# Routing slice cut on token rows by VectorE, first chunk's lookup readied early, other lookups moved among the pairs of the linear attention

## The reference, cut to what matters

```python
xn = (x - mu) * rsqrt(var + eps) * ln_gamma + ln_beta          # second norm, on LN(x)
tile_idx = argmax over 64 tiles, in the best cluster, of sign(xn) @ tile_sigs.T
x_slice = xn[8*tile_idx : 8*tile_idx + 8]                      # 8 numbers per token
tok_min, tok_max = x_slice.min(), x_slice.max()
tile_min, tile_max = min / max of these over all tokens of a tile     # over all 2048 tokens
u = clip((x_slice - tile_min[tile_idx]) / (tile_max - tile_min + 1e-8), 0, 1 - 1e-6)
gi = floor(16 * u)                                             # one of 16 cells
delta = (bases[tile, j, gi] + slopes[tile, j, gi] * x_local) * output_scale[tile]
out[token, 8*tile_idx + j] = delta[j]
```

## Time and profile before

| what | value |
|---|---|
| median of 3 runs | 2363.11 us (2361.16 to 2364.78) |
| the profiled execution | 2363.24 us, span of the trace 2361.5 us |
| PE busy | 2062.1 us, 87% of the span, 12078 matmuls |
| DVE busy | 1227.2 us, 52% |
| ACT busy | 746.9 us, 32% |
| POOL busy | 220.9 us, 9% |

### The profile page before, as it was taken

One profiled execution on the slowest core, in us unless ns is written; L12 is line 12 of the kernel. 1 busy time (PEld: TensorE's weight loads), 2 busy tenths in 40 slices (PEclk: granted clock), 3 DMA queues, 4 the chain that ended last, 5 costly groups with the idle time before them and its releaser, 6 DMA issues. The chain is left out here.

```text
span 2361.5 us, 29596 instructions
## 1 busy us (share of the span) xinstructions
PE 2062.1 (87%) x12078; PEld 987.3 (42%) x12078; DVE 1227.2 (52%) x2281; ACT 746.9 (32%) x1163; POOL 220.9 (9%) x164
## 2 busy tenths in 40 slices
PE   5885669697975499989999899999998999999998
PEld 3553233334343344434444444444444444444443
DVE  5554364757643455463666265644565356623332
ACT  4562231324341112322235223432244223511211
POOL 3630202120200000000000010001000000000000
PEclk7886769797966599999999999999999999999999
DMA  7224030302021222322111111111111111122321
GB/s 258 83 72 167 1 58 1 58 1 58 8 52 72 81 72 98 110 87 72 45 42 59 53 46 37 63 36 63 54 55 45 54 46 54 63 90 99 116 93 68
DMA packets 90978, 158.75 MB, mean 67 GB/s; under 512 B 44182, under 2 KB 55772, under 8 KB 86108
## 3 DMA queue, kind: packets, MB, share of 16 engines
q1 hardware_dynamic: 90844, 156.86, 20.7%
HBM read 128.52 MB, written 18.87 MB: 62 GB/s over the span
## 5 line engine op out<-in xcount | busy, mean ns | idle before, releaser
L1169 PE MATMUL ps<-arena 128*128 128x512 f16 (+1 forms) x4512 | 1018.3, 381 | 22.6 <-DVE arena L1932 12.9
L1169 PEld LDWEIGHTS ps<-arena 128*128 128x128 f16 x4512 | 436.4, 99 | 542.8 <-issue 48.5
L1877 PE MATMUL ps<-arena 128*128 128x512 f16 x1536 | 349.0, 383 | 29.5 <-DVE arena L1923 16.3
L1877 PEld LDWEIGHTS ps<-arena 128*128 128x128 f16 x1536 | 147.4, 98 | 207.4 <-issue 29.4
L1899 ACT ACTIVATE arena<-ps,arena 128x512 f32<-128x512 f32 x128 | 87.6, 684 | 362.4 <-PE ps L1169 362.1
L1932 DVE SCALAR_TENSOR_TENSOR arena<-arena,ps 128x512 f32<-128x512 f32 x128 | 87.8, 686 | 210.1 <-ACT arena L1899 209.5
L2486 ACT ACTIVATE arena<-ps 128x1024 f32<-128x1024 f32 (+3 forms) x128 | 90.1, 704 | 253.7 <-PE ps L2395 253.6
L2591 DVE CAST arena<-arena 128x1024 f16<-128x1024 f32 (+3 forms) x128 | 66.6, 520 | 149.8 <-ACT arena L2486 147.7
L2557 DVE TENSOR_REDUCE arena<-ps 128x2 f32<-128x256 f32 (+3 forms) x128 | 99.5, 819 | 65.1 <-PE ps L2339 65.1
L1960 DVE SCALAR_TENSOR_TENSOR arena<-ps,arena 128x512 f32<-128x512 f32 x64 | 44.0, 687 | 139.6 <-PE ps L1877 139.4
L1941 DVE SCALAR_TENSOR_TENSOR arena<-ps,arena 128x512 f32<-128x512 f32 x128 | 95.7, 748 | 39.5 <-PE ps L1169 39.3
(11 more groups left out here) (265 smaller groups left out, 2446.7 us busy)
## 6 DMA issues: line engine op xcount, KB each, us to landing
arena<-wug_dram SPq DMA_DIRECT2D x128, 512.0 KB, 3.3
arena<-wd_hi_dram SPq DMA_DIRECT2D x16, 1024.0 KB, 5.0
arena<-wd_lo_dram SPq DMA_DIRECT2D x16, 1024.0 KB, 7.2
arena<-arena SPq DMA_DIRECT2D x144, 64.0 KB, 2.1
wug_dram<-arena SPq DMA_DIRECT2D x4, 2048.0 KB, 15.4
arena<-_attn_hidden_states_dram SPq DMA_DIRECT2D x4, 1024.0 KB, 12.4
arena<-in_L_ffn_W_up_dram SPq DMA_DIRECT2D x8, 512.0 KB, 4.4
arena<-in_L_ffn_W_down_dram SPq DMA_DIRECT2D x4, 1024.0 KB, 7.7
```

What stands on the lines that cost most here:

```text
L1169: ins = pe.matmul(out, left[a](c), right[b](c), start=(at == 0), stop=(at == 3 * n - 1))
L1877: ins = pe.matmul(k.ps[:, bank, :], act[x][:, slot, cols], wd[y][:, f, :], start=(f == 0 and m == 0), stop=(f == 7 and m == 2))
```

## The change

1. **Slice on token rows.** `y` stays token-major and is not scaled. ACT takes the sign straight from the bank, with gamma as scale and beta as bias (4 activations fewer per chunk). The four spreading matmuls and the 16 gathering matmuls go. DVE multiplies each token row (128x512) by the one-hot broadcast over 8, and reduces it over the tiles to 8 numbers; the reduce reads elements 32 bytes apart. As the slice is of the unscaled row, PE fetches gamma and beta of the tile with four matmuls of 16 columns (two more DMAs put them into `table`), and DVE multiplies and adds them in `route_ends_vector`.
2. **Lookup of chunk 0 readied.** In both spline blocks the one-hot, its turn, the copy and the 256 columns of bases and slopes are done before the extremes are known; after them PE fetches three columns. The scaling of x is done ahead too, and in setup the wait for the two bias loads stands behind the norm's sums.
3. **Lookups of chunks 1 to 3 among the pairs**, in one bank (6), in three parts, at steps 3, 6, 8 and 11. The sums of the weighted values have one bank (5) instead of two. Everything of q and k stands one step earlier, and the refinement of the lengths comes before the last mask instead of after it.
4. **Values first.** In the feature stretch the values are made in blocks 0 to 3, the outputs from block 4 on. On SP the values' store and reads stand ahead of the last 12 feature copies.
5. Routing in the rounds: two picks at the end of a round, two at steps 1 and 2 of the next, the extremes at step 3 (before at step 1). The waits on registers go, POOL's loop is written out.

```diff
+def route_gain_tensor(k, pe, i, n, bank):
+    for u in range(TPC):
+        ins = pe.matmul(k.ps[:, bank, 256 + 2 * DSL * u:256 + 2 * DSL * (u + 1)], k.hot_t[:, u * P:(u + 1) * P],
+                        k.table[:, 260:276], start=True, stop=True)
 def route_sign_scalar(k, e, i, n, c, banks):
-    e.activation(y, token_columns(k.ps[:, banks[c % 2], :]), ACT.Identity, bias=k.beta[:, c:c + 1],
-                 scale=k.gamma[:, c:c + 1]).then_inc(s["r_y"], 1)
-    e.activation(token_columns(k.sgt[:, c, :]), y, ACT.Sign).then_inc(s["r_sign"], 1)
+    e.activation(k.sgt[:, c, :], k.ps[:, banks[c % 2], :], ACT.Sign, bias=k.beta[:, c:c + 1],
+                 scale=k.gamma[:, c:c + 1]).then_inc(s["r_sign"], 1)
-def route_pick_vector(k, V, i, n, c, banks):
-    e.tensor_tensor(y, token_columns(k.ps[:, banks[c % 2], :]), y, ALU.mult).then_inc(s["r_picked"], 1)
+def route_pick_vector(k, V, i, n, u):
+    V.link(e.tensor_tensor(y.rearrange("p (t j) -> p t j", j=DSL), y.rearrange("p (t j) -> p t j", j=DSL),
+                           bcast(hot.unsqueeze(2), [P, NTILE, DSL]), ALU.mult))
+    e.tensor_reduce(k.sliced[:, bass.ds(i * TPC + u, 1), :].squeeze(1), y.rearrange("p (t j) -> p j t", j=DSL), AXX, ALU.add)
 def route_ends_vector(k, V, i, n, bank):
+    V.link(e.tensor_tensor(cells, cells, gain[:, :, 0:DSL], ALU.mult))
+    e.tensor_tensor(cells, cells, gain[:, :, DSL:2 * DSL], ALU.add).then_inc(s["r_cut"], 1)
-    e.tensor_copy(k.sliced[:, bass.ds(i * TPC, TPC), :], cells).then_inc(s["r_cut"], 1)
...
-            "key": (2, 0), "hot": (2, 1), "mask": ((2, 2), (2, 2), (2, 3), (2, 3)), "slice": (3, 0), "ends": (3, 1)}
+            "key": (2, 0), "hot": (2, 1), "pick": ((2, 1), (2, 2), (2, 2), (2, 3)), "gain": (2, 2), "ends": (3, 0)}
...
+    sp.dma_start(k.table[:, 260:268], d["L0_ffn_ln_gamma"].rearrange("(t j) -> t j", j=DSL)).then_inc(s["param_in"], 16)
+    sp.dma_start(k.table[:, 268:276], d["L0_ffn_ln_beta"].rearrange("(t j) -> t j", j=DSL)).then_inc(s["param_in"], 16)
...
+def ready_cols_tensor(k, pe, ready, banks, parts):
+    pe.wait_ge(k.s["table_ready"], ready)
+    for u in range(TPC):
+        ins = pe.matmul(k.ps[:, banks[u], 256:259], k.oht[:, u * P:(u + 1) * P], k.table[:, 256:259], start=True, stop=True)
...
-SUM_BANK = (5, 6)
+SUM_BANK = 5
-LOOK_CELLS, LOOK_SLOPES, LOOK_BASES = 7, 5, 6
+LOOK_BANK = 6
-QK_AT = (1, 2, 4, 5, 7, 8)
-SPREAD_AT = 13
-REFINE_AT = 15
+QK_AT = (0, 1, 3, 4, 6, 7)
+SPREAD_AT = 12
+REFINE_AT = 14
+LOOK_START, LOOK_PLACE, LOOK_SLOPE, LOOK_VALUE = 3, 6, 8, 11
...
     def weighted(y):
-        if y % 4 == 0 and y >= 8:
-            pe.wait_ge(s["b_ot_lo"], TPC * now + y // 4 - 1)
+        if y % 4 == 0 and y:
+            pe.wait_ge(s["b_ot_lo"], TPC * now + y // 4)
...
     spread(k.qs, (0, 1, 0), slice(2, 4), slice(0, 2), s["b_qs"])
-    sp.wait_ge(s["b_f_lo"], 6 * i + 6)
-    spread(k.qs, (0, 1, 0), slice(4, 6), slice(2, 4), s["b_qs"])
     sp.wait_ge(s["b_v_in"], TPC * (i + 1))
...
+    sp.wait_ge(s["b_f_lo"], 6 * i + 6)
+    spread(k.qs, (0, 1, 0), slice(4, 6), slice(2, 4), s["b_qs"])
...
         @block.tensor
             setup_tensor(k, pe)
+            ready_rows_tensor(k, pe, 0, 1, ROWS_BANK)
             minmax_tensor(k, pe, 1, "")
-            apply_turn_tensor(k, pe, 0, 1, LOOK_CELLS)
-            look_rows_tensor(k, pe, 0)
+            ready_cols_tensor(k, pe, 1, ROWS_BANK, 3)
```

More of the change, by code:

```diff
@@ L570, in route_tensor @@
     route_hot_tensor(k, pe, i, n, banks[0])
-    for c in range(KC):
-        route_mask_tensor(k, pe, i, n, c, banks)
-    route_slice_tensor(k, pe, i, n, bank)
+    route_gain_tensor(k, pe, i, n, bank)
 def route_scalar(k, e, i, n, banks):
@@ L621 @@
 KEY_BANK = 6
+READY_BANK = 7
 VECTORS = 70
@@ L814, in setup_tensor @@
                 route_hot_tensor(k, pe, i, 1, ROUTE_BANK[0])
-            for c in range(KC):
-                i = route_now(n, r, "mask", c)
-                if i is not None:
-                    route_mask_tensor(k, pe, i, 1, c, ROUTE_BANK)
-            i = route_now(n, r, "slice")
+            i = route_now(n, r, "gain")
             if i is not None:
-                route_slice_tensor(k, pe, i, 1, KEY_BANK)
+                route_gain_tensor(k, pe, i, 1, KEY_BANK)
+            if (n, r) == (GROUPS - 1, 3):
+                apply_turn_tensor(k, pe, 0, 1, READY_BANK)
     pe.wait_ge(s["had_lo"], 4 + 4 * GROUPS)
@@ L1317, in value @@
             return
-        if u < 2 and now is not None:
-            pe.wait_ge(s["b_res"], TPC * now + u + 3)
         if u >= 2:
@@ L1500, in b_scalar @@
         norm_write_scalar(k, e, look, look, k.h, range(TPC), s["n_h"])
+    if body:
+        for c in range(KC):
+            route_sign_scalar(k, e, back, route, c, BACK_BANK)
+    if look is not None:
         for c in range(KC):
@@ L1561, in b_vector @@
     route = 1 + NCH
-    cells, slopes, bases = look_rows(k)
     def mask(y):
@@ L1678, in b_vector @@
     if look is not None:
-        spline_slope_vector(k, V, slopes)
-    residual(1)
+        for u in range(TPC):
+            scatter_tile_vector(k, V, u)
+    value(1)
     low(1)
@@ L1716, in b_vector @@
     if body:
-        for c in range(KC):
-            route_pick_vector(k, V, back, route, c, BACK_BANK)
+        route_choice_vector(k, V, back, route, BACK_KEY)
+        route_pick_vector(k, V, back, route, 0)
+        route_pick_vector(k, V, back, route, 1)
     if i == NCH - 1:
@@ L2731, in _ @@
                 b_pool(k, pool, i)
-            with pool.Fori(0, NCH) as i:
+            for i in range(NCH):
                 c_pool(k, pool, i)
```

426 lines of the change are left out of this document (216 added, 210 removed).

## The result

The changed kernel takes 2309.62 us (median of 4 runs, 2308.93 to 2311.19) against 2363.86 us before on the same chip: ratio 0.9776, 95% interval 0.9761 to 0.979. That is 54 us less. The forecast was 28 less, 2335 us with a range down to 2315: the sign was right, the gain was half of what came, and the time fell out of the range. The profiled execution of the changed kernel took 2309.18 us, its span 2307.3.

A forecast was written before the change was run, and what follows sets the result against it. PE bounds from 815 us on, unchanged; before that, cross-engine waits. Setup -7.2, first lookup -12.5, first round +4.5, rounds 0 to 3 +4.3, -0.2, -2.5, -3, last part -11.2: -27.8 from 2363.24, so 2335 us, range 2315 to 2355.

The forecast's parts named there:

- The feature stretches: Stretches ending with SP's copies and values: 0 gained in the first round, then 4.2, 8.7 and 6.2 us.
- block 4 at 28.4: Feature stretch: block 4 done 28.4 us after the start, as DVE has scaling, scatter, sum and statistics in the first four blocks.
- Reordering SP's queue saves little by itself: End of the feature stretch: the last 12 copies only take the place of the values.
- The pair stretches: Lookups and single-bank waits among the pairs: 8.5 us longer in rounds 0 and 1, 3.7 in round 2.
- 18 us of DVE meet 16 of PE: Round 2's pairs, steps 1 to 4: picks and late extremes on DVE, +3.7 us with the bank and the refinement.
- Setup: Start of the kernel: slice work leaves PE, mixes start sooner, two more parameter loads cost 0.8; -7.2 us in all.
- The first lookup: Chunk 0's lookup after setup: only three columns fetched after the extremes, ready rows uncovered on PE; -12.5 us.
- the last part: Last routing and second lookup: shorter picks and extremes, readied lookup, scaling done ahead; -11.2 us.
- the pick's price: Multiply 0.69 and strided reduce 1.02 us on DVE, 1.75 us a pick with the gap.
- the first projections: First round, with no pairs: cold small matmuls and DVE's place in the rotation chain cost 4.5 us.
- Round 3: Slice leaves between masks and signs, longer picks and later extremes stand on DVE: -3 us, bounds -6 to +1.
- SP gives nothing: Rival: last copies wait for block 6, feature stretches keep 63, 67 and 53 us; 2354 us, chance 0.15.

The follow-up runs named there:

- e6: Kernel before without the lookups of chunks 1 to 3 in the feature stretch, a memset of their deltas instead: 2336.1 us, ratio 0.9896.
- e1: Changed kernel with SP's store and reads of the values moved back behind the last 12 feature copies: 2317.22 us, ratio 0.9806.
- e2: Kernel before with only SP's new order, values' store and reads ahead of the last 12 copies: 2371.17 us, ratio 1.0036.
- e4: Changed kernel without the lookups of chunks 1 to 3 among the pairs, their deltas zero, still one sums bank: 2286.58 us, ratio 0.968.
- (d): Edit to the changed kernel: in rounds 2 and 3 the extremes stand behind the rotation of step 3; not timed alone, part of e10, e11, e12.
- e8: Changed kernel with POOL's mixing of the later down-weight quarters held until the slice of chunks 0 to 2 is cut: 2320.64 us, ratio 0.9826.
- e7: Changed kernel with every pick's reduce reading contiguous neighbours, summing other elements but as many: 2292.9 us, ratio 0.9714.
- e9: Changed kernel with each pick's product written with a 256-byte step and its reduce reading side by side: 2308.35 us, ratio 0.9767.
- (b): Edit to the changed kernel: in setup PE turns the extremes before the ready rows, DVE scales x behind the extremes; not timed alone.
- (c): Edit to the changed kernel: SP stores the values right behind the first 12 feature copies; not timed alone, part of e10, e11, e12.
- e10: Changed kernel with (b), (c), (d) and POOL's later mixing waiting for the extremes of chunks 0 to 2: 2308.27 us, ratio 0.9759.
- e11: The kernel of e10 with the permuted product write of e9 added: 2312.91 us, ratio 0.9787.
- e12: Changed kernel with (b), (c) and (d) only, POOL mixing where it did: 2292.85 us, ratio 0.9714.

## Why the prediction was wrong, and where it held

**The feature stretches (the failed step).** What failed is the price of SP's copies, 0.85 us where 0.64 was measured, and with it the reading that SP's queue is what ends the stretch. The prediction said: "At 0.85 us a copy: 12 copies 10.2", and "block 4 at 28.4", so 28.4 + 10.2 + 3.6 + 4.3 + 10.2 + 2.1 = 58.8 us (58.9 in its text). With the measured terms of round 0 the same sum is 24.7 + 7.7 + 3.2 + 4.1 + 7.6 + 1.7 = 49.0, and 48.9 was measured. Of the 9.8 us between the two sums 5.1 are the price of 24 copies, 3.7 block 4, 1.0 the store, the reads and the landing. The 0.85 came from dividing a merged row by its count; the row held 8.2 us besides three times 7.62: 0.7 within the first 12 copies, 2.8 behind them and 4.7 before the last 12. The last two are waits for DVE, and they are what the moved lookup shortens: with the lookups left out (e6) block 6 was ready sooner and the same 19.3 us followed. With that price I also misread the bound: the earlier trace rows looks like a queue that is busy for 31 us, and was a queue that waits for DVE. Splitting it would have put round 0 5 us lower.

The price does not explain every round. The misses were 11.5, 10.0, 6.1 and 0.8 us in rounds -1 to 2. For round -1 I had no gain at all, since "block 4 comes later still"; it came 26.1 us after the start (299.5), and the stretch gave 11.5. For round 1 I let the routing end at 58 us without a sum; its last pick ended at 542.13, 52.7 us after the start. In round 2 the near hit (45.9 for 46.7) is luck: behind block 4 my terms come to 30.4 us, which leaves 16.3 for block 4. It took 20.7 and the rest 25.2, so the two errors cancel. Why block 4 was 3.7 us early in round 0 was not tested.

**"Reordering SP's queue saves little by itself"** held: e1 puts it at 7 to 8 of 54 us, e2 shows it as a loss without the early values.

**The pair stretches** held in rounds 0 and 1 (57.3 and 59.4 for 58), and by the waits that the forecast named. It had 1.9 us for `weighted(8)`, 2.5 for `weighted(12)` and 2.1 for `weighted(15)`; round 0 shows 2.08, 2.33 and 1.77, round 1 2.08, 2.35 and 1.79:

```profile
362.78 0.68 PE L1311 MATMUL ps<-arena 128*32 128x64 f32 x16 [2.08 <-DVE arena L1607]
375.82 0.65 PE L1311 MATMUL ps<-arena 128*32 128x64 f32 x16 [2.33 <-DVE arena L1607]
380.54 0.66 PE L1311 MATMUL ps<-arena 128*32 128x64 f32 x16 [1.77 <-DVE arena L1599]
```

Without the lookups (e4) the first is gone, the second is 1.14 and the third stays at 2.03, and the stretches are 7 us shorter. A wait of 1.40 us for the rotation (L1329 at 364.86) was in no term. Round 2 was mis-sized, 10.4 for 3.7: the rotation of step 3 stands behind the picks, the second norm's sums and the late extremes on DVE, one of those picks is the slow one of 548.28, and PE waits for it:

```profile
562.16 2.05 PE L1329 MATMUL ps<-arena 128*128 128x512 f32 x2 [5.97 <-DVE arena L1615]
```

The prediction had counted that "18 us of DVE meet 16 of PE" and had not followed the one chain in it. (d) takes 4.6 of it away.

**Setup** was 3.4 us better than forecast, but not by its steps. From one chunk's mix to the next it had 2.4, 2.7, 1.5 and 1.5 us gained, and the traces show 1.6 lost, then 5.6, 4.5 and 2.1 gained. In the second and third PE's busy time fell by 7.2 and 7.4 us (35.61 to 28.45, 36.84 to 29.43), at a granted clock of 0.92 and 0.89 for 0.87 and 0.83; how much of the extra gain is the clock is not separated. The loss at chunk 0 was in no step: a pick's multiply has both inputs in SBUF, and three of them stood still beside POOL, 4.4 us together (1.93 + 2.77 + 1.72 less 3 x 0.68). The kernel before had no such operation there; its picks read PSUM. The Trainium skill ("SBUF — State Buffer", section "Who interferes with whom") states this: a DVE instruction with two SBUF inputs contends with a GpSimd instruction that reads SBUF, a copy or `tensor_scalar` can, a reduce never does, and one with a single SBUF input outside the two-port modes doesn't. The rows of e8 agree in all four (L542 at 2.81 us, L540 at 2.20, a reduce, L543, at 1.04 and evictions out of PSUM at 0.68 and 0.69 beside POOL). It was a rule to weigh against this change, and the prediction did not.

**The first lookup (12.7 for 12.5) and the last part (11.8 for 11.2)** held by their steps, and so did the pick's price, 1.75 us (1.07 and 0.68). e7 is in line with 0.38 us for each pick on the path: 9.9 expected, 11.7 found without the first projections. Round 3 (4.3 for 3) and the first projections (-5.3 for -4.5) came close, the latter perhaps by luck: without a lookup that stretch took 35.0 us at a granted clock of 0.96 (e4, e6), 37.2 at 0.90 (e2) and 38.8 at 0.85 (before), so the stretch moves with the clock by nearly as much as the forecast.

Of the rivals, "SP gives nothing" was near the truth on SP's order (7 to 8 us) and wrong on the feature stretches, since it took for granted that the end depends on SP. No rival had the feature stretches shorter than forecast; every rival on that side was about pairs or picks.

## What to carry to other kernels

A merged row of a queue can hold its waits: divide it by its count only after cutting it at the instructions that it waits for, and ask what the queue waited for before pricing the queue. Taking work off the engine that feeds a queue gave 18.5 us in three feature stretches here (e6, where it is left out and not moved), reordering the queue alone lost 8 (e2). When an operation goes from a PSUM to an SBUF operand, look at what POOL runs beside it, and before holding POOL back, look at when its result is needed.

## What the runs showed of the hardware that I had not expected

- A DVE multiply of 128x512 float32 with both inputs in SBUF takes 0.68 us alone and up to 2.77 us beside a POOL `tensor_tensor` (2.81 in e8); a DVE `tensor_scalar` of 4 columns 2.20 instead of 0.17 (e8). A reduce and an eviction out of PSUM are not touched.
- A step in a write cost about what a step in a read did: a multiply with a 256-byte step in its output 1.04 us (e9), a reduce with a 32-byte step in its input 1.07, either contiguous 0.68 or 0.69 (e7).
- The granted clock moves a stretch of the same instructions by some us. The first projections without a lookup took 35.0 us at 0.96, 37.2 at 0.90 and 38.8 at 0.85. Round 2's feature stretch took 45.9 us at 0.83 in the changed kernel, and 49.8, 47.1 and 47.2 at 0.71, 0.76 and 0.76 in the three runs with (b), (c) and (d) (e10, e11, e12). So part of what (c) and (d) took away came back there as a lower clock; that they lowered it fits the three runs and is not shown by one of its own.
